# Context MLP and routing of a fused transformer pair: ScalarE normalises the token tiles with a scale and a bias per token, GpSimd makes the bias

## The reference

```python
x = x + _L0_xattn_ref(_layernorm(x), ctx_1024, ctx_1024, mask, ...)   # cross attention
x = x + _L0_ffn_ref(_layernorm(x), ...)                               # gated attention, 4 of 16 heads
x = x + _L1_xattn_ref(_layernorm(x), ctx_1024, ctx_1024)              # context MLP
x = x + _L1_ffn_ref(_layernorm(x), ...)                               # top-1 of 8 experts
...
def _layernorm(x, axis=-1, eps=1e-05):
    m = jnp.mean(x, axis=axis, keepdims=True)
    v = jnp.var(x, axis=axis, keepdims=True)
    return (x - m) / jnp.sqrt(v + eps)

def _L1_xattn_ref(x, w1, w2):          # w1 = w2 = the context: 77 rows of 256 per batch
    h = jnp.einsum('eth,efh->etf', x, w1)
    g = jax.nn.gelu(h, approximate=True)
    return jnp.einsum('etf,efh->eth', g, w2)
...
logits = jnp.einsum('bsh,he->bse', x, w_router)   # routing, on the normalised x
probs = jax.nn.softmax(logits, axis=-1)
sel = jnp.argmax(probs, axis=-1)
```

## Time and profile before

| | us |
|---|---|
| median of 3 runs | 738.28 |
| the three runs | 734.52, 738.28, 740.21 |
| the profiled execution | 740.46 |
| its span in the profile | 738.7 |

### The profile page before, as it was taken

How to read it: one execution, slowest core, us unless ns; L and a number is a source line. 1 busy time by engine, 2 the same in 40 slices (tenths; PEclk the granted TensorE clock), 3 DMA queues, 4 the chain that set the end, 5 groups by cost and what they waited for, 6 DMA issues and landing times. The chain is left out here.

```text
span 738.7 us, 12022 instructions
## 1 busy us (share of the span) xinstructions
PE 586.2 (79%) x3622; PEld 507.3 (69%) x3623; DVE 497.5 (67%) x960; ACT 292.3 (40%) x536; POOL 312.2 (42%) x261
## 2 busy tenths in 40 slices
PE   4578999964397999999999986777006989989985
PEld 4468888953275898888888874457004878867874
DVE  5598888857406889898889857574702566566562
ACT  2144445412035787787878830223100121111120
POOL 4335344427012443343444312045470295699144
PEclk9699999995599999999999998865556999999998
DMA  6112111100342313222131002833425034044000
GB/s 212 29 34 53 30 28 29 29 1 7 87 116 49 81 43 76 55 63 67 43 87 44 1 1 82 295 104 150 163 101 180 16 147 180 7 161 157 29 14 4
DMA packets 28727, 56.47 MB, mean 76 GB/s; under 512 B 4410, under 2 KB 15675, under 8 KB 26634
## 3 DMA queue, kind: packets, MB, share of 16 engines
q1 hardware_dynamic: 24810, 49.64, 22.4%
q0 software_dynamic: 1776, 4.23, 1.6%
q10 hardware_dynamic: 2096, 2.05, 0.9%
HBM read 31.58 MB, written 8.21 MB: 54 GB/s over the span
## 5 line engine op out<-in xcount | busy, mean ns | idle before, releaser
L880 POOL TENSOR_SCALAR h_p<-h_p,h_rs 128x1024 f32<-128x1024 f32 x64 | 72.1, 1126 | 131.9 <-DVE h_rs L972 131.8
L979 DVE TENSOR_REDUCE h_nmx<-h_psS 128x1 f32<-128x1024 f32 x64 | 78.1, 1221 | 22.3 <-PE h_psS L1070 21.0
L959 DVE TENSOR_TENSOR h_pTl<-h_psT,h_pTh 128x512 fp32r<-128x512 f32 x128 | 81.5, 678 | 4.4 <-ACT h_pTh L907 4.4
L907 ACT CAST h_pTh<-h_psT 128x512 fp32r<-128x512 f32 x128 | 69.3, 590 | 29.6 <-PE h_psT L1030 29.4
L929 ACT ACTIVATE h_p<-h_psS,h_nmx 128x1024 f32<-128x1024 f32 x64 | 72.2, 1128 | 17.7 <-DVE h_nmx L979 17.7
L1041 PE MATMUL h_psO<-h_pTh,h_vs 128*128 128x256 f32 x256 | 70.0, 307 | 3.1 <-DVE h_oT L967 2.3
L308 POOL TENSOR_TENSOR a_p<-a_p,a_rs 128x616 f32<-128x616 f32 x32 | 39.0, 1219 | 74.7 <-DVE a_rs L355 74.7
L1030 PE MATMUL h_psT<-ident,h_p 128*128 128x128 f32 x512 | 67.4, 273 | 1.3 <-DVE h_pTl L959 1.2
L1030 PEld LDWEIGHTS h_psT<-ident,h_p 128*128 128x128 f32 x512 | 59.2, 140 | 11.2 <-issue 3.3
L1041 PE MATMUL h_psO<-h_pTl,h_vs 128*128 128x256 f32 x256 | 63.7, 282 | 0.0
L1500 POOL TENSOR_TENSOR wl<-wst,wh 128x1024 fp32r<-128x1024 f32 (+1 forms) x18 | 56.0, 3110 | 2.7
(11 more groups left out here) (262 smaller groups left out, 1475.0 us busy)
## 6 DMA issues: line engine op xcount, KB each, us to landing
wst<-in_m_w SPq DMA_DIRECT2D x16, 1024.0 KB, 6.0
bias<-in_m_b SPq DMA_DIRECT2D x8, 640.0 KB, 8.8
h_kh<-h_hi SPq DMA_DIRECT2D x32, 128.0 KB, 2.4
h_kl<-h_lo SPq DMA_DIRECT2D x32, 128.0 KB, 2.4
rows<-c_blank SPq DMA_DIRECT2D x1, 3250.0 KB, 18.7
xg<-rows SPq DMA_DIRECT2D x1, 2990.0 KB, 11.1
a_qs<-a_qhi SPq DMA_DIRECT2D x16, 128.0 KB, 2.3
a_qs<-a_qlo SPq DMA_DIRECT2D x16, 128.0 KB, 2.3
```

Of the source, the lines that this page charges most:

```text
L880: pool.tensor_scalar(pr[:, u % 4], pr[:, u % 4], rs[:, u:u + 1], 0.0, ALU.mult, ALU.add).then_inc(pn_ready, 1)
L907: act.copy(pTh[u // QP % 2][:, hf * HK:(hf + 1) * HK, u % QP * P:(u % QP + 1) * P], psT[hf][:]).then_inc(pT_hi, 1)
L959: vec.tensor_tensor(pTl[u // QP % 2][part], psT[hf][:], pTh[u // QP % 2][part], ALU.subtract).then_inc(pT_lo, 1)
L979: vec.tensor_reduce(nmx[:, u:u + 1], psS[u % 2][:], AX.X, ALU.max, negate=True).then_inc(max_ready, 1)
```

## The change

ACT computes x * rstd + shift with shift = -mean * rstd, as one activation (Identity) with a scale and a bias per token. DVE makes -mean in one small instruction beside each variance + eps, and POOL multiplies it by rstd right behind the power, at both places where statistics are made. The normalise calls leave DVE's queue and stand in ACT's: 0 and 1 first, 2 between copy_x(1) and tanh(0), 3 between copy_x(2) and tanh(1), 4 before tanh(2), 5 before tanh(3), 6 behind copy_x(5), 7 behind copy_x(6) and before high(3).

```diff
             for n in range(NC):                       # gated_attention, POOL
                 pool.wait_ge(var_ready, n + 1)
-                pool.tensor_tensor(t["rstd"][:, n * CH:(n + 1) * CH], t["rstd"][:, n * CH:(n + 1) * CH], mhalf[:],
-                                   ALU.pow)
+                part = slice(n * CH, (n + 1) * CH)
+                link(pool.tensor_tensor(t["rstd"][:, part], t["rstd"][:, part], mhalf[:], ALU.pow))
+                pool.tensor_tensor(t["shift"][:, part], t["shift"][:, part], t["rstd"][:, part], ALU.mult)
...
+                    vec.tensor_scalar(t["shift"][:, n * CH:(n + 1) * CH], t["mv"][:, n * CH:(n + 1) * CH, 0], -1.0,
+                                      None, ALU.mult)
                     vec.tensor_scalar(t["rstd"][:, n * CH:(n + 1) * CH], t["mv"][:, n * CH:(n + 1) * CH, 1], EPS,
                                       None, ALU.add).then_inc(var_ready, 1)
...
             def power(n):                             # context_mlp, POOL
                 pool.wait_ge(var_ready, n + 1)
-                pool.tensor_tensor(rstd4[:, n * CH:(n + 1) * CH], rstd4[:, n * CH:(n + 1) * CH], mhalf[:],
-                                   ALU.pow).then_inc(rstd_ready, 1)
+                part = slice(n * CH, (n + 1) * CH)
+                link(pool.tensor_tensor(rstd4[:, part], rstd4[:, part], mhalf[:], ALU.pow))
+                pool.tensor_tensor(shift4[:, part], shift4[:, part], rstd4[:, part], ALU.mult).then_inc(rstd_ready, 1)
...
         def _(act):                                   # context_mlp, ACT
+            def normalise(i):
+                n = i % NC
+                s_, r_ = (shift, rstd) if i < NC else (shift4, rstd4)
+                if i >= NC:
+                    act.wait_ge(rstd_ready, n + 1)
+                if i >= 2:
+                    act.wait_ge(xT_ps, i - 1)
+                for j in range(CH):
+                    t_ = n * CH + j
+                    ins = act.activation(xn[:, i % 2, j], x_all[:, t_, 0:D], ACT.Identity, bias=s_[:, t_:t_ + 1],
+                                         scale=r_[:, t_:t_ + 1])
+                ins.then_inc(xn_ready, 1)
...
+            normalise(0)
+            normalise(1)
             copy_x(0)
             square(0)
             copy_x(1)
+            normalise(2)
             tanh(0)
-            for n in range(1, NC):
-                square(n)
-                copy_x(n + 1)
-                tanh(n)
-                if n >= 2:
-                    high(n - 2)
+            square(1)
+            copy_x(2)
+            normalise(3)
+            tanh(1)
+            square(2)
+            copy_x(3)
+            normalise(NC)
+            tanh(2)
+            high(0)
+            square(3)
+            copy_x(NC)
+            normalise(NC + 1)
+            tanh(3)
+            high(1)
             copy_x(NC + 1)
+            normalise(NC + 2)
             high(2)
             copy_x(NC + 2)
+            normalise(NC + 3)
             high(3)
             copy_x(NC + 3)
...
         def _(vec):                                   # context_mlp, DVE
-            def normalise(i):
...
-                    ins = vec.tensor_scalar(xn[:, i % 2, j], x_all[:, t_, 0:D], m_[:, t_, 0:1], r_[:, t_:t_ + 1],
-                                            ALU.subtract, ALU.mult)
...
+                vec.tensor_scalar(shift4[:, n * CH:(n + 1) * CH], mv4[:, n * CH:(n + 1) * CH, 0], -1.0, None, ALU.mult)
                 vec.tensor_scalar(rstd4[:, n * CH:(n + 1) * CH], mv4[:, n * CH:(n + 1) * CH, 1], EPS, None,
                                   ALU.add).then_inc(var_ready, 1)
-            normalise(0)
-            normalise(1)
             gelu(0)
-            normalise(2)
             gelu(1)
-            normalise(3)
             for n in range(NC):
                 update(n)
                 if n + 2 < NC:
                     gelu(n + 2)
-                normalise(NC + n)
 
             vec.wait_ge(consts, 1)
+            vec.wait_ge(rstd_ready, NC)
```

More of the change, by code:

```diff
@@ L883, in _ @@
                     split_v(i + 1)
+            link = Link(pool, sem("h_pool"))
             pool.memset(mhalf[:], -0.5).then_inc(half_ready, 1)
@@ L1123, in context_mlp @@
         stats = sb("c_stats", [P, 2, CH, 6])
-        mv, rstd = t["mv"], t["rstd"]
+        rstd, shift, shift4 = t["rstd"], t["shift"], sb("c_shift4", [P, T])
         mhalf, mv4, rstd4 = sb("c_mhalf", [P, CH]), sb("c_mv4", [P, T, 2]), sb("c_rstd4", [P, T])
@@ L1266, in _ @@
             link = Link(vec, dve)
-            def normalise(i):
[L1269 to L1276, removed]
-                    ins = vec.tensor_scalar(xn[:, i % 2, j], x_all[:, t_, 0:D], m_[:, t_, 0:1], r_[:, t_:t_ + 1],
-                                            ALU.subtract, ALU.mult)
-                ins.then_inc(xn_ready, 1)
             def gelu(n):
@@ L1665, in program @@
         t["ctxT"], t["ctxs"], t["wr"] = sb("ctxT", [P, B, KD, L]), sb("ctx", [L, B, D]), sb("wr", [P, KD, NE])
-        t["mv"], t["rstd"] = sb("mv", [P, T, 2]), sb("rstd", [P, T])
+        t["mv"], t["rstd"], t["shift"] = sb("mv", [P, T, 2]), sb("rstd", [P, T]), sb("shift", [P, T])
         t["table"], t["slot"] = sb("table", [1, TABLE], I32), sb("slot", [P, T], I32)
```

## The result

The changed kernel takes 743.00 us (median of 5 runs, 742.02 to 744.87) against 738.28 (median of 5, 734.52 to 740.21): a ratio of 1.0083, 95% interval 1.0056 to 1.0109. It is slower by 0.8%, inside the 1% of the forecast, and 0.5 us from the predicted 742.5. The forecast was +4.2 us; the medians differ by 4.7, and the ratio stands for about 6. Its profiled execution took 742.02, with a span of 740.3.

What follows compares the result with a forecast made beforehand. No engine is full; a chain of short pieces bounds the stage, so normalise's latency and queue place count. Steps (a) to (e) +4.5, round 6 +1.98, tail -2.3: +4.2 us, 742.5 us, range 738.5 to 748.5.

Steps and rivals of the forecast that it cites:

- (a): Start of the stage: POOL's product and DVE's negation delay it by +0.33 us, bounds 0.1 to 1.1.
- (b): Round 0: its normalise is the first thing on the chain and slower on ACT, +0.70 us.
- (c): Round 2's normalise stands before tanh(0): tanh(0) +3.01 us; slack takes 0.5, leaving back-multiplication 0 at +2.5.
- (d): Round 3's normalise stands before tanh(1): +1.98 us, less DVE's 1.31 ahead of update(0), which comes +3.2 later.
- (e): Two cycles, rounds 4 and 5 ahead of tanh(2) and tanh(3): 8.37 us each for 7.70, update(2) +4.5.
- (f): Round 6: normalise behind copy_x(5) on ACT loses its cover, another 1.98 us, transposition 6 at +6.5.
- (g): Round 7: the last normalise no longer takes DVE's 5.44 us; -2.3 us in the tail, softmax at +4.2.
- the rival with a clock that falls early: PE's clock falls one or two cycles earlier, 2.8 us per cycle: 745.3 or 748.1 us; chance 0.22.
- free operands: Rival: scale and bias cost nothing on ACT, six normalises each 0.75 us less: 738.0 us; chance 0.07.
- free scale: Case: the scale alone costs nothing on ACT, 6 x 0.37 us less: 740.3 us, the forecast's lower bound.
- activations without overlap: Case: ACT's normalise instructions don't overlap, four take 2.36 us: 744.2 us, the forecast's upper bound.
- POOL too late: Rival: POOL's late subtractions stand beside DVE's softmax, one more step waits up to 2.4 us: 744.9 us; chance 0.07.

Runs made afterwards that it cites:

- before_lows_late: Kernel before, with POOL's subtractions low(6) and low(7) moved behind the scatter instead of ahead of it: 745.34 us, ratio 1.0109.
- before_no_stall7: Kernel before, with high(2) moved behind copy_x(6) on ACT, so POOL's subtraction starts after the last normalise: 736.12 us, ratio 0.9979.
- products4: Changed kernel with three more small products on POOL behind the last power before the stage: 750.91 us, executed once.

## Why the prediction was right

Times from the stage's start, before and changed; predicted without (a):

| step | before | changed | measured | predicted |
|---|---|---|---|---|
| (b) copy_x(0) starts | 3.50 | 4.20 | +0.70 | +0.70 |
| (c) tanh(0) | 10.86 | 13.59 | +2.73 | +2.68 |
| (c) back-multiplication 0 | 12.80 | 14.98 | +2.18 | +2.2 |
| (d) update(0) | 19.07 | 22.02 | +2.95 | +2.9 |
| (e) update(2) | 35.08 | 40.12 | +5.04 | +4.2 |
| (f) transposition 6 | 43.09 | 50.01 | +6.92 | +6.2 |
| (g) softmax | 59.37 | 63.75 | +4.38 | +3.9 |

The mechanism was right: where normalise stands in ACT's queue, and what that adds to the chain, step by step. The price of one normalise was right to a nanosecond or two, and scale and bias together cost what was charged for them. (b), (c), (d) hold to 0.1. Step (a) was wrong: from DVE's last mean and variance to the stage it is 2.32 us before and 2.34 changed, so negation and product together cost 0.02 and not 0.33, under even the lower bound of 0.1. In (e) the cycle at full clock was right (8.38), and the excess of 0.8 is the clock, but for 0.1: it fell in the first cycle here (9.72 us), a cycle earlier than in the profile before, and came back. It took 1.34 us of one cycle and spared the 0.6 that the kernel before loses in its second (8.31 us for 7.70). That is in part the rival with a clock that falls early, and one of the prediction's own signs of being wrong, PEclk at another level in other cycles than before.

That the change moved the clock isn't shown, though. The order before does the same in two of its four executions: before_lows_late and before_no_stall7, alike in these cycles, have 8.45 and 8.41 us in the first and 7.85 and 7.89 in the second, with the clock down from about 478 to 485. The changed order fell early in all three of its executions (9.72, 9.67 and 10.36 us). The rival's price was about right: in products4 the second cycle, at the low level throughout, took 10.99 us, 2.6 more than 8.38, for the 2.8 predicted.

(f) and (g) hold: 1.88 and -2.54 for 1.98 and -2.3. The errors of the two steps, -0.3 and +0.8, partly cancel, and the whole, 0.5 us off, came closer than its worst term. That is luck, as the five runs before alone lie 5.7 us apart. The ends of the range, 738.5 to 748.5, are a little inside the prediction's own working, which gives 738.3 to 749.

Of the rivals, free operands and free scale are refuted by 590 ns for one activation, against 407 without both, and activations without overlap by 2.07 us for four. POOL too late did not happen (softmax to scatter 16.34 us). What I did not see, though the rows were there, is that the loss lay in the order and not in the move: tanh ahead of normalise could have been costed from the same rows.

## What to carry to other kernels

When work moves to another engine, cost its latency at the place where it enters that queue: 2 us ahead of tanh were on the chain in four rounds, and 2 us behind it were free. What the move off VectorE was worth here was the stall beside GpSimd, not the load, and most of that was to be had by moving one instruction that sets GpSimd going (before_no_stall7); so look first at who starts whom. Work that is postponed past a barrier's last user isn't gone: look at what each queue, and the barrier itself, must now wait for.

## What the hardware showed that I had not expected

A DVE normalise (one SBUF tensor, two per-partition scalars) that started inside a POOL subtraction stood still for most of it: four took 2.71, 2.76, 5.42 and 5.44 us, and 1.37 to 1.39 without. Where the normalise had started first, it kept its 1.37 us and the subtraction took 3.20 or 3.15 us for 2.35. PE's clock took different courses through the same instructions from execution to execution: the changed kernel's stage took 63.75 us in one and 66.85 in another (products4), and the first cycle of the order before took 7.70 us in two executions and 8.4 in two more. And the end of a block left room for just one small product of 0.28 us behind POOL's last power.
